# A one-core decoder layer: opening reordered, Newton roots in place of two table-switched square roots, one turned norm moved, batch 0 quantised by VectorE

## What is computed

```
x = x + attn(layernorm(x))            # 16 heads of 64, causal
x = x + xattn(layernorm(x), ctx, ctx) # 16 heads of 8, two softmaxes of half heads, a1 - lam*a2
x = x + ffn(layernorm(x))             # act_quant to 8 bits, ternary weights, depthwise conv (3 taps), silu
layernorm(x) = (x - mean) / sqrt(var + 1e-5)
act_quant(x) = clip(round(x * s), -128, 127) / s,  s = 127 / max|x|
```

## Time and profile before

| | us |
|---|---|
| median of 3 runs | 338.84 (338.49 to 346.44) |
| the profiled execution itself | 340.07 |
| its span, first to last instruction | 338.3 |
| TensorE busy | 298.5 (88%) |
| VectorE busy | 214.6 (63%) |
| ScalarE busy | 200.9 (59%) |
| GpSimd busy | 141.5 (42%) |
| mean granted TensorE clock | 0.945 of full |

### The profile page before, as it was taken

One profiled execution on the slowest core, in us unless ns is written; L12 is line 12 of the kernel. 1 busy time (PEld: TensorE's weight loads), 2 busy tenths in 40 slices (PEclk: granted clock), 3 DMA queues, 4 the chain that ended last, 5 costly groups with the idle time before them and its releaser, 6 DMA issues.

```text
span 338.3 us, 6590 instructions
## 1 busy us (share of the span) xinstructions
PE 298.5 (88%) x2446; PEld 186.4 (55%) x2446; DVE 214.6 (63%) x471; ACT 200.9 (59%) x490; POOL 141.5 (42%) x229
## 2 busy tenths in 40 slices
PE   1697889899999989897999998899998879994993
PEld 0464766556666677564666774344454432362772
DVE  3844587887777715866776479378877860047643
ACT  2476447677777733866778308658875674415333
POOL 4624538884477824843466000612263631000230
PEclk9999599999999999999999999589999995999698
DMA  7800000000000000000000000000000000000001
GB/s 285 309 24 1 2 1 2 3 2 0 3 2 3 2 0 2 3 0 2 2 0 4 2 0 2 1 0 2 0 2 1 0 3 0 0 0 2 0 23 41
DMA packets 4835, 6.17 MB, mean 18 GB/s; under 512 B 834, under 2 KB 3650, under 8 KB 4676
## 3 DMA queue, kind: packets, MB, share of 16 engines
q1 hardware_dynamic: 4516, 5.42, 4.5%
q10 hardware_dynamic: 288, 0.33, 0.3%
HBM read 5.23 MB, written 0.52 MB: 17 GB/s over the span
## 4 chain that ended last, share of the span: by engine, by line
PE 73%; DVE 12%; ACT 9%; issue 3%; DMA 1%; ACTq 0%; DVEq 0%
PE bank L679 65%; PE bank L752 5%; ACT pr L503 4%; DVE nmax L1279 3%; ACT pT L503 1%; PE bank L806 1%; PE bank L907 1%; DVE xn L1223 1%; DVE qk L1324 1%; DMA x_sb<-in_x 1%; ACT pT L600 1%; ACT L600 1%; ACT L461 1%; DVE stats L1210 1%; PE bank L963 1%
## 5 line engine op out<-in xcount | busy, mean ns | idle before, releaser
L600 ACT ACTIVATE pT<-bank 128x512 f32<-128x512 f32 (+1 forms) x80 | 44.5, 600 | 31.9 <-PE bank L679 31.4
L1324 DVE TENSOR_REDUCE qk<-bank 128x4 fp32r<-128x616 f32 x64 | 49.1, 796 | 20.9 <-PE bank L679 20.8
L324 POOL TENSOR_SCALAR pr<-pr,pinv 128x256 f32<-128x256 f32 (+2 forms) x96 | 46.0, 496 | 33.5 <-DVE pinv L1287 33.4
L503 ACT ACTIVATE pr<-bank,nmax 128x256 f32<-128x256 f32 (+2 forms) x96 | 44.3, 478 | 20.7 <-DVE nmax L1279 20.4
L679 PE MATMUL bank<-qs 64*128 64x256 f32 (+3 forms) x256 | 49.4, 469 | 3.7 <-ACT pr L503 3.7
L1279 DVE TENSOR_REDUCE nmax<-bank 128x2 f32<-128x512 f32 (+2 forms) x48 | 31.7, 687 | 14.8 <-PE bank L679 14.8
L679 PE MATMUL bank<-pT,v_sb 128*64 128x128 f32 (+2 forms) x320 | 38.4, 385 | 0.0
L324 POOL TENSOR_SCALAR pT<-pT,pinv 128x512 f32<-128x512 f32 x32 | 21.7, 692 | 30.3 <-DVE pinv L1287 30.3
L679 PE MATMUL bank<-qk,km 64*128 64x512 f32 x64 | 29.3, 471 | 4.2 <-ACT pT L600 4.2
L1295 DVE COPY pT<-bank 128x512 f32<-128x512 f32 (+1 forms) x32 | 30.4, 949 | 1.3 <-PE bank L752 1.3
L679 PE MATMUL bank<-km,qk 64*128 64x308 f32 x128 | 29.0, 373 | 2.2 <-DVE qk L1324 2.1
(11 more groups left out here) (181 smaller groups left out, 601.5 us busy)
## 6 DMA issues: line engine op xcount, KB each, us to landing
pT<-in_wqk SPq DMA_DIRECT2D x1, 1024.0 KB, 6.0
cw_sb<-in_cw SPq DMA_DIRECT2D x1, 768.0 KB, 9.1
x_sb<-in_x SPq DMA_DIRECT2D x2, 256.0 KB, 5.1
pT<-in_wv SPq DMA_DIRECT2D x1, 512.0 KB, 6.7
wo_sb<-in_wo SPq DMA_DIRECT2D x1, 512.0 KB, 7.3
out<-x_sb SPq DMA_DIRECT2D x8, 64.0 KB, 1.6
onT<-in_consts ACTq DMA_DIRECT2D x1, 256.0 KB, 6.2
pT<-in_xwk SPq DMA_DIRECT2D x1, 256.0 KB, 7.2
```

The costliest lines, as they stand in the source:

```text
L324: nc.gpsimd.tensor_scalar(d, d, pinv[:, t, a:a + 1], 1.0, ALU.mult, ALU.mult).then_inc(norm_done, 1)
L503: nc.scalar.activation(prob[r][:, a, at:at + w], bank[:, SP[k % 2] + a, at:at + w], ACT.Exp, bias=nmax[:, t, a:a + 1], accum_out=psum[:, t ...
L600: nc.scalar.activation(px[rows, i, :], bank[rows, (ST0, ST1)[i % 2], :], ACT.Exp, scale=SD ** -0.5).then_inc(xexp_done, 1)
L1324: nc.vector.tensor_reduce(m, s_in, AX.X, ALU.max, negate=True).then_inc(round_done, 1)
```

## The change

- **Opening.** `turn_norm(1, 2)` moves from ahead of the value tiles to behind `scores(0, 0)`. The four `stack_keys` go between value tiles 8 and 15, one bank (PJ0) for all four. On ScalarE the splits of context and cross key weights come ahead of batch 1's square root, the big copy of the query and key weights comes later, and the key copies go between value copies. The mask casts go from VectorE to GpSimd.
- **Roots.** `root_of_variance` of batch 1 (G=0) and of batch 0 (G=6) are gone from ScalarE. In their place are Newton steps for 1/sqrt(v) on 128x4 numbers: 14 instructions on GpSimd for batch 1 and 11 on VectorE for batch 0, each waiting for the one before.
- **Second turned norm** in the cross attention: from G=1 to G=2, where `stack_queries(4)` and `query_parts(4)` move behind it.
- **Batch 0's quantisation** (8 instructions) goes from GpSimd to VectorE. Its statistics, root, centring and scale take new places in G=6.
- `conv(0)` runs after the last score tile of G=7, no longer between them.

The diff, its core:

```diff
-            for p in range(NPAIR):
-                pool.wait_ge(wqk_high, 1 if p < 2 else 2)
-                low(wqk_l[:, p, :, :], wqk_sb[:, p, :, :], wqk_h[:, p, :, :], wqk_low)
+            pool.wait_ge(wqk_high, 1)
+            low(wqk_l[:, 0, :, :], wqk_sb[:, 0, :, :], wqk_h[:, 0, :, :], wqk_low)
+            pool.wait_ge(ld_mask, 16)
+            nc.gpsimd.tensor_copy(mask_b[:, :, :].rearrange("p a b -> p (a b)"), mask_st[:, 0:2 * P]).then_inc(cast_pool, 1)
+            nc.gpsimd.tensor_copy(sel_b[:, :, :].rearrange("p a b -> p (a b)"), mask_st[:, 2 * P:4 * P]).then_inc(cast_pool, 1)
+            low(wqk_l[:, 1, :, :], wqk_sb[:, 1, :, :], wqk_h[:, 1, :, :], wqk_low)
...
-            pool.wait_ge(asplit_h, 3)
+            pool.wait_ge(asplit_h, 2)
...
+            for p in range(2, NPAIR):
+                pool.wait_ge(wqk_high, 2)
+                low(wqk_l[:, p, :, :], wqk_sb[:, p, :, :], wqk_h[:, p, :, :], wqk_low)
+            pool.wait_ge(asplit_h, 3)
...
+            def inverse_root(b, k):
...
+                v, y = std[:, NT * b:NT * b + NT], rstd[:, NT * b:NT * b + NT]
+                half, step = nroot[:, 0, :], nroot[:, 1, :]
+                pool.wait_ge(var_ready, k)
+                link(nc.gpsimd.tensor_scalar(y.bitcast(I32), v.bitcast(I32), -0.5, ROOT_SEED, ALU.mult, ALU.add))
+                link(nc.gpsimd.tensor_scalar(half, v, -0.5, None, ALU.mult))
+                settle()
+                for _ in range(3):
+                    link(nc.gpsimd.tensor_tensor(step, half, y, ALU.mult))
+                    settle()
+                    link(nc.gpsimd.tensor_tensor(step, step, y, ALU.mult))
+                    settle()
+                    link(nc.gpsimd.tensor_scalar(step, step, 1.5, None, ALU.add))
+                    settle()
+                    link(nc.gpsimd.tensor_tensor(y, step, y, ALU.mult))
+                    settle()
...
             def norm_apply(b):
-                pool.wait_ge(rstd_done, 1)
...
+                ps = bank[:, PJ0, 0:B * S2].rearrange("p (b n) -> p b n", b=B)
...
+            act.wait_ge(ld_cx, 16)
+            nc.scalar.copy(ctx_h, ctx_sb).then_inc(asplit_h, 1)
+            act.wait_ge(ld_xk, 32)
+            nc.scalar.copy(xwk_h, xwk_sb).then_inc(asplit_h, 1)
...
-            nc.scalar.copy(wqk_h[:, 2:NPAIR, :, :], wqk_sb[:, 2:NPAIR, :, :]).then_inc(wqk_high, 1)
-            turned_norm(1, 2, ST1)
...
             def value_copy(i):
...
             exps(0, 0)
+            turned_norm(1, 2, ST1)
             value_copy(2)
             value_copy(3)
-            act.wait_ge(ld_cx, 16)
-            act.wait_ge(ld_xw, 16 * 9)
-            nc.scalar.copy(ctx_h, ctx_sb).then_inc(asplit_h, 1)
-            nc.scalar.copy(xwk_h, xwk_sb).then_inc(asplit_h, 1)
-            nc.scalar.copy(xwq_h[:, :, :], xwq_sb).then_inc(asplit_h, 1)
+            nc.scalar.copy(wqk_h[:, 2:NPAIR, :, :], wqk_sb[:, 2:NPAIR, :, :]).then_inc(wqk_high, 1)
             exps(0, 1)
+            act.wait_ge(ld_xw, 16 * 7)
             value_copy(4)
+            stacked_keys(0)
             value_copy(5)
...
             exps(0, 2)
             value_copy(6)
+            stacked_keys(2)
             value_copy(7)
-            for g in range(NG):
-                stacked_keys(g)
+            stacked_keys(3)
+            nc.scalar.copy(xwq_h[:, :, :], xwq_sb).then_inc(asplit_h, 1)
...
-                if G + 2 < B * NG:
+                if G == 2:
+                    turned_norm(1, 4, PJ0)
+                elif G + 2 < B * NG:
...
                 if G >= 1:
...
-                if G == 6:
-                    root_of_variance(0, 5)
-                if G == 1:
-                    turned_norm(1, 4, PJ0)
+                if G == 2:
+                    query_parts(G + 2)
                 if G == 5:
...
                 if G == 7:
...
-                cross_exps(G, range(4, 7))
-                if G == 0:
-                    root_of_variance(1, 4)
-                cross_exps(G, range(7, 10))
+                cross_exps(G, range(4, 10))
...
-                if g >= 2:
-                    pe.wait_ge(k_act, 2 * (g - 1))
...
+                if g == 0:
+                    pe.wait_ge(q_done, 1)
+                else:
+                    pe.wait_ge(k_act, 2 * g)
+                mm3(bank[:, PJ0, 0:B * S2].rearrange("p (b n) -> p b n", b=B), xwk_h[:, g, :],
...
-            turn_norm(1, 2, ST1)
...
             value_tile(0)
...
             value_tile(2)
             value_tile(3)
-            pe.wait_ge(cast, 4)
+            pe.wait_ge(cast_pool, 2)
             scores(0, 0)
+            turn_norm(1, 2, ST1)
...
                 value_tile(u)
...
             scores(0, 1)
-            for u in range(8, 12):
-                value_tile(u)
+            value_tile(8)
+            pe.wait_ge(asplit_h, 2)
+            pe.wait_ge(asplit_l, 3)
+            stack_keys(0)
+            value_tile(9)
+            value_tile(10)
...
+            value_tile(11)
             scores(0, 2)
-            for u in range(12, 16):
-                value_tile(u)
...
-            pe.wait_ge(asplit_h, 3)
-            pe.wait_ge(asplit_l, 4)
-            pe.wait_ge(v_dve, 8)
-            pe.wait_ge(v_act, 8)
-            for g in range(NG):
-                stack_keys(g)
+            value_tile(12)
+            stack_keys(2)
+            value_tile(13)
+            value_tile(14)
+            stack_keys(3)
+            value_tile(15)
...
+            pe.wait_ge(v_dve, 7)
...
-                if G + 2 < B * NG:
+                if G == 2:
+                    pe.wait_ge(qb1_done, 3)
+                    turn_norm(1, 4, PJ0)
+                elif G + 2 < B * NG:
...
-                if G == 1:
-                    pe.wait_ge(xq_act, 8)
-                    turn_norm(1, 4, PJ0)
+                if G == 2:
+                    stack_queries(4)
                 if G == 5:
...
-                    conv(0, [0])
                 cross_scores(G, 7)
...
-                else:
-                    conv(0, [1])
                 cross_scores(G, 8)
...
-                else:
-                    conv(0, [2])
                 cross_scores(G, 9)
...
+            conv(0)
...
-            nc.vector.tensor_copy(ident_b[:, :], con[:, C_ID:C_ID + P]).then_inc(cast, 1)
...
+            dve.wait_ge(wv_high, 1)
+            low(wv_l, wv_sb, wv_h, wv_low)
+            keys(0)
...
-            dve.wait_ge(wv_high, 1)
-            low(wv_l, wv_sb, wv_h, wv_low)
-            keys(0)
-            turned_norm_low(1, 2, ST1)
-            dve.wait_ge(ld_mask, 16)
-            nc.vector.tensor_copy(mask_b[:, :, :].rearrange("p a b -> p (a b)"), mask_st[:, 0:2 * P]).then_inc(cast, 1)
-            nc.vector.tensor_copy(sel_b[:, :, :].rearrange("p a b -> p (a b)"), mask_st[:, 2 * P:4 * P]).then_inc(cast, 1)
             value_copy(0)
             value_copy(1)
             row_max(0, 0)
+            turned_norm_low(1, 2, ST1)
             value_copy(2)
             value_copy(3)
...
             row_max(0, 1)
-            value_copy(4)
-            value_copy(5)
-            row_max(0, 2)
-            value_copy(6)
-            value_copy(7)
-            invert_sums(0, 1)
-            invert_sums(0, 2)
...
-            settle()
...
-            for g in range(NG):
-                stacked_key_rows(g)
...
-            nc.vector.tensor_scalar(wmean[:, :], bank[:, PT, 0:2], 1.0 / (FH * C), Q_EPS, ALU.mult,
...
+            value_copy(4)
+            stacked_key_rows(0)
+            value_copy(5)
+            row_max(0, 2)
+            stacked_key_rows(1)
+            value_copy(6)
+            invert_sums(0, 1)
+            stacked_key_rows(2)
+            value_copy(7)
+            invert_sums(0, 2)
+            stacked_key_rows(3)
+            nc.vector.tensor_copy(ident_r[:, :], con[:, C_ID:C_ID + P]).then_inc(cast, 1)
...
+            settle()
...
+            dve.wait_ge(wqk_low, NPAIR)
...
             for n in range(1, STEPS):
...
-                dve.wait_ge(std_ready, k)
-                nc.vector.reciprocal(rstd[:, NT * b:NT * b + NT], std[:, NT * b:NT * b + NT]).then_inc(rstd_done, 1)
-                dve.wait_ge(rstd_done, k - 3)
...
+                v, y = std[:, NT * b:NT * b + NT], rstd[:, NT * b:NT * b + NT]
+                half, step = nroot[:, 0, :], nroot[:, 1, :]
+                dve.wait_ge(var_ready, k)
+                link(nc.vector.tensor_scalar(y.bitcast(I32), v.bitcast(I32), -0.5, ROOT_SEED, ALU.mult, ALU.add))
+                link(nc.vector.tensor_scalar(half, v, -0.5, None, ALU.mult))
+                settle()
+                for _ in range(3):
+                    link(nc.vector.tensor_tensor(step, half, y, ALU.mult))
+                    settle()
+                    link(nc.vector.tensor_tensor(step, step, y, ALU.mult))
+                    settle()
+                    link(nc.vector.scalar_tensor_tensor(y, step, 1.5, y, ALU.add, ALU.mult))
+                    settle()
...
             def centre(ts):
...
```

(23 more changed lines are left out.)

50 lines of the change are left out of this document (28 added, 22 removed).

## The result

The changed kernel takes 327.36 us (median of 4 runs, 325.83 to 329.19) against 338.66 for the kernel before on the same chip. The ratio is 0.9665, 95% interval 0.9592 to 0.9738. The forecast was 325.0 with a range of 321 to 332. The profiled execution took 328.66 (span 326.8), which is 11.4 less than the 340.07 of the profile before. (A ratio leaves out executions more than 1.5% above the fastest of their kernel, and a median here is over all of them, so the two differ for a kernel whose clock varies.)

A forecast was written before the change was run, and what follows sets the result against it. TensorE was taken as the bound nearly everywhere, losing time to waits and the half clock after them. 340.07 less 5.9 (G=0 to G=2), 5.0 (G=6, G=7, conv(0)) and 3.4 (opening) gave 325.8; forecast 325.0, range 321 to 332.

The forecast's parts named there:

- the stall behind `stack_queries`: G=2: exponentials 4 and on start one activation pair later, priced at less than one exponential of 0.60 us.
- The cover: G=0 to G=2: GpSimd's root, 3.8 us, and the normalisations finish before TensorE's transposition; room 7.7 us, cost none.
- With no stall the clock stays up: G=0 and G=1: without the 2.8 us of loads and root on ScalarE, G=1 takes 8.73 us as G=2 did.
- This holds if the clock does not fall at the 1.6 us gap: Before G=7: condition for 5.0 us less; TensorE idles 1.6 us in one piece, and a clock fall costs 4.0.
- the clock falls at the gap before G=7: Rival, 25%: half clock behind TensorE's gap before G=7 costs 4.0 us, time 329.0.
- The nearest row chosen: Gap before G=7: likened to 141 to 145 us, TensorE busy 2.47 of 4.0 us, where the clock did not fall.
- the term for GpSimd's queue: Opening: query weights split before the first probabilities are multiplied, so step 0's turns wait; 0.9 us lost.
- its 1.3: Opening: without a gap from 11.3 us on, TensorE's clock may rise up to 2.6 us earlier, worth 1.3 us.
- The opening gave something: Answers a rival, 10%: ScalarE bounds the opening and new waits eat its earlier start, 328.4 us.
- the exponentials did move up: Answers a rival, 3%: roots leave ScalarE but exponentials wait for something else, no stretch gets shorter, 338.8 us.
- no step of a root came near 0.55: Roots: GpSimd exceeds its room from 0.55 us a step; rival, 3%, slower than before from 0.80 on.
- each table switch holds ScalarE longer than the rows show: Rival, 2%: each of four table switches holds ScalarE another 1.38 us, and that goes too, 319.5 us.

The follow-up runs named there:

- e9: Changed kernel with nine Newton steps in place of three in GpSimd's root of batch 1: 333.6 us, ratio 0.9678 to the kernel before.
- e11: Changed kernel with batch 1's turned norm in G=1 again, its root still on GpSimd: 331.91 us, ratio 0.963 to the kernel before.
- e3: Changed kernel with conv(0) between the scores of G=7 and batch 0's root on GpSimd: 323.31 us, ratio 0.9502 to the kernel before.
- e8: Changed kernel with four unused matmuls on TensorE just ahead of G=7's first score: 325.99 us, ratio 0.9565 to the kernel before.
- e4: Changed kernel with the old opening on all engines: 331.93 us, ratio 0.9725 to the kernel before.
- e6: Changed kernel with batch 1's square root on ScalarE in G=0 again, with table loads: 330.61 us, ratio 0.9684 to the kernel before.
- e1: Changed kernel with conv(0) between the scores of G=7, as before the change: 323.1 us, ratio 0.9497 to the kernel before.
- e2: Changed kernel with batch 0's root on GpSimd in place of VectorE: 322.25 us, ratio 0.9483 to the kernel before.
- e7: Changed kernel with batch 0's square root on ScalarE in G=6 again, with table loads: 334.61 us, ratio 0.9817 to the kernel before.
- e5: Kernel before with the new opening alone: 333.37 us, ratio 0.9782 to the kernel before.
- e10: Changed kernel with six Newton steps in place of three in VectorE's root of batch 0: 330.89 us, ratio 0.9745 to the kernel before.
- e0: The changed kernel measured again, without edits: 327.24 us, ratio 0.9577 to the kernel before.

## Why the prediction was right in its sum and wrong in one term

**G=0 to G=2, forecast 5.9 less, measured 6.3.** G=0 came at 9.89 (9.9 forecast), G=1 at 8.74 (8.7), G=2 at 9.41 (9.8): the stall behind `stack_queries` was 0.4 smaller. The cover held, as e9 and e11 show from both sides. GpSimd's steps were 0.29 us apart, not 0.274. "With no stall the clock stays up" held in ten of the eleven profiles that have the new G=0, and in e3 it did not. The root started 7.7 us into G=0 and took 4.0; with the 3.8 to spare its room was 7.8, and the forecast had 7.7.

**G=6, G=7 and `conv(0)`, forecast 5.0 less, measured 0.9.** This is the term that failed, and the step that failed is "This holds if the clock does not fall at the 1.6 us gap". G=6 was 9.87, 0.6 shorter than forecast, since the gap was 0.84 and not 1.6. VectorE's root started 5.6 us into the group, not 5.9, and took 2.0, not 2.3. Then the clock fell: G=7 took 10.80 and `conv(0)` 4.86, where 8.0 and 2.6 were forecast. The rival with 25%, "the clock falls at the gap before G=7", came in. Its price was right, 4.0 forecast, and 25.5 - 21.0 = 4.5 between the profiles of the changed kernel and e8. Its chance was too low. Six profiles have this code for G=6, G=7 and `conv(0)` unchanged: the changed kernel's two, e4, e6, e9 and e11. They take 25.5, 23.9, 24.0, 25.5, 24.0 and 21.0 us, so the forecast 21.1 came once in six.

The nearest row chosen, that of 141 to 145 with 2.47 us busy of 4.0, was the wrong neighbour: the new stretch has 1.87 of 3.4 busy, for TensorE waits again (0.69) behind the first scores of G=7. And the gap is the smaller part of it. In two of the six profiles the clock fell there, at 269.1 in the changed kernel, and in five it fell in the second half of G=7, behind the wait of 0.45 at 274.95, ahead of the late `conv(0)`. That second fall had no place in the working. e1 keeps the gap and holds 0.985 in all five executions; e8 fills it, and four of its six still lie between 0.966 and 0.976, though where their clock fell no trace shows; e2 takes the gap away and lies between 0.976 and 0.989. Together they show that the whole stretch, from the gap through G=7, is thin for TensorE, and that either filling its second half (e1) or shortening VectorE's part (e2) gains 3 us. What decides in a single execution whether the clock falls stays open.

The other half of this term, that ScalarE's table loads go from G=6, was worth more than the profiles of the changed kernel show: to put them back costs 8.2 us by the ratios (e7), nearly all of it by the clock.

**Opening, forecast 3.4 less, measured 5.1 in the profile, 5.0 (e4) and 7.4 (e5) by the ratios, 3 at equal clock.** The waits were sized well: 0.83 and 1.93. The start was 2.4 earlier, where 2.6 was read off the rows. Most of the 1.7 that was missed is the term for GpSimd's queue, 0.9: it did not come. The split of the query weights ended at 36.2 and the first normalisation at 37.3, ahead of ScalarE's `qs` at 38.8, which set the turn as it had before the change, with 0.78. The rest is clock, 0.7 more than the 2.2 of the sum. In the profile before, TensorE's 512-column matmuls start 0.43 us apart until about 18.1 and 0.23 apart from there on; in the changed one the change comes at about 12.8 (the clock column reads 1.00 there in both, so the steps are the evidence). That is 5.3 earlier, of which 2.4 go with the earlier start. So 1.3 us behind the first value tile ran at half and not 4.2, worth 1.5. And of 6.8 us at half later on, 6.2 of them busy, 3.4 stayed, worth 1.4. The forecast had counted the first of these twice: a rise that comes earlier by no more than the start leaves the same work at half, so its 1.3 had no ground, and what came was a rise earlier than that.

**The tail, forecast 0, measured 0.8 longer.** It lies at the very end: TensorE's last block of the output starts 4.0 us ahead of the span's end, where it was 3.3. In the twelve profiles of the experiments it is 2.7 to 3.2, so this belongs to the one execution and not to the change.

**Sum.** 5.1 + 6.3 + 0.9 - 0.1 - 0.8 gives 11.4 against 14.3. Two errors, one of -4.1 and one of +1.7, partly cancel. That the sum lies nearer to the truth than its terms is luck.

**The other rivals.** The opening gave something, the exponentials did move up, and no step of a root came near 0.55. That each table switch holds ScalarE longer than the rows show falls with e6 and e7: with both switches put back, 2.82 us from the first load to the next exponential, as in the earlier trace rows. The section "What ACT_TABLE_LOAD costs" of "ScalarE: Activation LUTs" in the Trainium skill adds a drain of 1380 ns; here no drain beyond the load shows. For small instructions, VectorE's 0.16 us busy and 0.20 apart agree in size with the fixed cost in the TRN2 errata of "VectorE: DVE Perf Modes" in the Trainium skill. It mattered: e10 shows that such a step costs its full 0.20 when it stands on the path. No run took the quantisation back to GpSimd or parted the opening's edits, so what each of these is worth alone is not shown.

## What to carry to other kernels

Moving a tiny chain off a busy engine pays only where its new engine has room: such a root was free on GpSimd and cost its full length on VectorE, ahead of an operation that TensorE waits for. When a change takes filler work away from a stretch paced by another engine (here `conv(0)` out of G=7), count the clock as a term with both signs, and look at several executions, since one profile shows only one place of the fall. The better version is e2 or e1, not their sum: by the ratios they can't be told apart.

## What the hardware showed that I had not expected

- One program, one chip: mean granted clock from 0.950 to 0.985 and spans from 321.5 to 332.3 us in the six executions of e0, with the same instructions. Stretches at half clock in the cross attention lasted from 3.4 to 20.5 us.
- Waits of 1.81 us (e6), 1.33 (e7) and 0.84 with 0.69 behind it (changed kernel) were followed by half clock in the profiles; one of 2.19 (e11, G=1) and one of 1.95 with 1.19 behind it (e0, opening) were not. In e3 the clock fell in G=0 for 10.3 us with TensorE busy for 2.83 of the 3.4 us ahead and no wait over 0.40. The length of a single wait doesn't tell what the clock does.
- A chain of 128x4 instructions runs at 0.20 us a step on VectorE and 0.29 on GpSimd, each with its wait for the one before.
